# Layer norms on GpSimd: (y - mean) * rstd instead of y * rstd + (-mean * rstd), and one fence fewer per norm

## The chip, the core and the metric

The kernel runs on one core of a Trainium2 chip. The core has TensorE (matmuls), VectorE (DVE), ScalarE (ACT), GpSimd (POOL), and SyncE (SP), which here issues the DMAs. Each has an instruction queue of its own, worked off in order; they meet through semaphores. The metric is the device time of one execution in microseconds.

## The reference

The input x is [64, 128, 256] fp32 (64 graphs of 128 nodes with 256 features), adj a [64, 128, 128] integer mask. First comes a masked attention with 8 heads, `x = norm(x + relu(attention(x)) @ Wo)`. Then three GNN layers, each for every graph:

```python
scores = si[:, :, None] + sj[:, None, :] + attn_b[l]      # si, sj = x @ two halves of attn_w[l]
attn = softmax(where(mask, leaky_relu(scores), -inf))
h = layernorm(x + attn @ x, g1[l], beta1[l])
ff = gelu(h @ W1[l] + b1[l]) @ W2[l] + b2[l]
x = layernorm(h + ff, g2[l], beta2[l])
```

and at the end `out = norm(x0 + x)`, with x0 the result of the attention. Every norm is `(y - mean) / sqrt(var + 1e-5)` over the 256 features.

## The kernel before, in words

The 64 graphs are worked in groups of 4 (GROUP), so there are 16 groups. A tile of a group is [128 nodes, 4 graphs, 256 features]. The first stage ("attention") goes through the 16 groups. The second ("GNN") has 48 steps: t = 0 to 15 is layer 1, 16 to 31 layer 2, 32 to 47 layer 3 (the last). x goes from layer to layer through DRAM (`hist`): a step loads its group's x and stores the new one.

There are four kinds of norms, all on GpSimd, each for the 4 graphs of a group at once: after the attention (`ln_group`, tiles y, mv, xo; 16 times), norm 1 (`ln_attention`, from y1 to n1, then hb = n1 * g1 + (beta1 + b2); 48 times), norm 2 (`ln_ffn`, from y2 to norm, then * g2, + beta2 into xo; 48 times), and in the last layer the final norm (`final_norm`, fin; 16 times). DVE makes means and variances (bn_stats, bn_aggr) and puts them as (mean, variance) pairs into mv, mv1, mv2, mv3. GpSimd then runs `layernorm_on_pool` (lines 145 to 158): variance + eps (148), -mean (149), power -0.5 (151), the product -mean * rstd (153), a fence, and four big `tensor_scalar` instructions, one per graph of 256 elements a partition, y * rstd + (-mean * rstd) (156). `hold_pool` (lines 140 to 143) is a fence: a wait, followed by a small tensor_tensor on one element, which goes ahead of an instruction that reads a scalar per partition. One stands before line 148 (on the semaphore of mv), one before line 156; in ln_attention a further one is on hT_made.

The order of each engine's work in a GNN step t is written out by hand:
- GpSimd (`body`, line 781 on): norm 1 and hb of step t+1, in the last layer the final norm of t-1, norm 2 and xo of t.
- TensorE: transposes of the probabilities of t+1 (line 799), FFN 1 of t in 8 parts (line 45), with the aggregation of t+1 between them (807), FFN 2 of t in 4 blocks (line 834), in the middle of the third of which n1 of t+1 is transposed (821). A block of FFN 2 needs the bank which `residual2` on DVE (line 1003) has read two blocks before.
- DVE: the low parts of gelu (1011), residual 1 and its statistics of t+1, the attention sums of t+3 (`attention_sums`, line 940, two instructions for each of 4 graphs) between the calls of residual2 (1003), the low part of hT of t+1 (1016), the statistics of y2 (1007) and at the end mv2 (1101). The first attention sum of t+3 waits for its loads (g_ld), and residual2 of block 0 stands behind it.
- SyncE, layers 1 and 2: `load_ahead(t)` waits for y1 of t+1 and issues the four loads of step t+3 (x, mask, attn_w, attn_b; lines 123 to 128), `store_x(t)` waits for x_out, that is for xo of t, and stores it (line 689). So load_ahead(t) stands behind store_x(t-1). In the last layer store_out takes the place of store_x.
- ACT: gelu (917, 918), the exponentials (890, 891), hT (904, 905).

The matmuls are made from high and low parts of fp32 values, three products each.

Of the kernel before, what the change touches and what calls it, by code (L numbers as in the profile page):

```python
# [27 lines left out]
ALU = mybir.AluOpType  # L28
ACT = mybir.ActivationFunctionType

P = 128
GROUP = 4
EPS = 1e-5
# [16 lines left out]
def gnn_kernel(nc, x_in, adj, Wq, Wk, Wv, Wo, attn_w, attn_b, W1, b1, W2, b2, g1, beta1, g2, beta2, out):  # L50
    B, N, D = x_in.shape
# [27 lines left out]
    with ExitStack() as whole:  # L79
# [6 lines left out]
        sb, sems = tensor_maker(whole), sem_maker(whole)  # L86
# [6 lines left out]
        affine = sb("affine", [P, L, 5, D])  # L93
        b2_rows = sb("b2_rows", [P, L, D])
        half_neg = sb("half_neg", [P, GROUP])
        w1_raw = sb("w1_raw", [P, KT, F])
        w2_raw = sb("w2_raw", [P, FT, D])

        y = [sb(f"y{i}", [P, GROUP, D]) for i in range(2)]
        mv = [sb(f"mv{i}", [P, GROUP, 2]) for i in range(2)]  # L100
        inv = sb("inv", [P, 4, GROUP])
        xo = [sb(f"xo{i}", [P, GROUP, D]) for i in range(2)]

        XW = D + 2
# [6 lines left out]
        mv_out, ln_chain, ln_out = sems("mv_out", "ln_chain", "ln_out")  # L111
# [28 lines left out]
        def hold_pool(e, sem, value):  # L140
            e.wait_ge(sem, value)
            n = holds["pool"] = holds["pool"] + 1
            e.tensor_tensor(fence_pool[:, n:n + 1], half_neg[:, 0:1], half_neg[:, 0:1], ALU.add)  # L143

        def layernorm_on_pool(e, chain, n0, stats, inv, y, dest, done=None):


            e.tensor_scalar(inv[:, 0, :], stats[:, :, 1], EPS, None, ALU.add).then_inc(chain, 1)
            e.tensor_scalar(inv[:, 1, :], stats[:, :, 0], -1.0, None, ALU.mult).then_inc(chain, 1)
            e.wait_ge(chain, n0 + 1)  # L150
            e.tensor_tensor(inv[:, 2, :], inv[:, 0, :], half_neg[:], ALU.pow).then_inc(chain, 1)  # L151
            e.wait_ge(chain, n0 + 3)
            e.tensor_tensor(inv[:, 3, :], inv[:, 1, :], inv[:, 2, :], ALU.mult).then_inc(chain, 1)
            hold_pool(e, chain, n0 + 4)
            for j in range(GROUP):
                last = e.tensor_scalar(dest[:, j, :], y[:, j, 0:D], inv[:, 2, j:j + 1], inv[:, 3, j:j + 1],  # L156
                                       ALU.mult, ALU.add)
            last.then_inc(chain if done is None else done, 1)

        def ln_group(e, t, par):  # L160

            hold_pool(e, mv_out, t + 1)
            layernorm_on_pool(e, ln_chain, 4 * t, mv[par], inv, y[par], xo[par], ln_out)
            e.wait_ge(ln_out, START + t + 1)


        with ExitStack() as ctx:
            sb = tensor_maker(ctx, "att_")
# [109 lines left out]
            @block.gpsimd  # L278
            def _(e):
                e.memset(ident[:], 0.0).then_inc(eye_made, 1)  # L280
                e.wait_ge(eye_made, 1)
                e.affine_select(out=ident[:], in_=ident[:], compare_op=ALU.not_equal, fill=1.0, base=0,
                                pattern=[[-1, P]], channel_multiplier=1).then_inc(ident_set, 1)
                e.memset(half_neg[:], -0.5).then_inc(eye_made, 1)
                e.sem_inc(ln_out, START)
                e.wait_ge(eye_made, 2)
                e.wait_ge(ident_set, 1)

                def make_masks(q1, par, t1):

                    hold_pool(e, x_ld[par], 32 * (q1 + 1))
                    e.tensor_scalar(mask[par][:], adjl[par][:], 0.0, MASKED, ALU.is_equal, ALU.mult).then_inc(masks_made, 1)
                    e.tensor_scalar(adj_f[:], adjl[par][:], 1.0, None, ALU.mult).then_inc(eye_added, 1)
                    e.wait_ge(eye_added, 2 * t1 + 1)
                    for j in range(GROUP):
                        ins = e.tensor_tensor(eye_sum[:, j, :], adj_f[:, j, :], ident[:], ALU.add)
                    ins.then_inc(eye_added, 1)
                    hold_pool(e, eye_added, 2 * t1 + 2)
                    hold_pool(e, mask1_st[par], START + 16 * q1)
                    e.tensor_scalar(mask1[par][:], eye_sum[:], 0.0, MASKED, ALU.is_le, ALU.mult).then_inc(masks_made, 1)  # L300

                make_masks(0, 0, 0)

                e.wait_ge(const_ld, 16 * (5 + 3 * L))
                e.tensor_tensor(affine[:, :, 2, :], affine[:, :, 1, :], b2_rows[:], ALU.add).then_inc(aff_set, 1)

                def body(q, par, a1, a2):
                    t = 2 * q + par
                    if a1:
                        e.wait_ge(masks_made, 2 * (t + 1))  # L310
                        e.wait_ge(peaked, GROUP * t + 1)
                        make_masks(q + (par + 1) // 2, 1 - par, t + 1)
                    if isinstance(t, int) and t == NG - 1:
                        return
                    e.wait_ge(stored[par], START + 16 * q)
                    ln_group(e, t, par)

                steps(e, body)
# [270 lines left out]
        with ExitStack() as ctx:  # L589
            sb = tensor_maker(ctx, "gnn_")  # L590
# [138 lines left out]
            @block.gpsimd  # L729
            def _(e):  # L730
                for par in range(2):
                    e.memset(x[par][:, :, D:XW], 1.0).then_inc(x_ones, 1)
                e.wait_ge(stored[1], START + 16 * (NG // 2 - 1))
                ln_group(e, NG - 1, 1)
                e.sem_inc(norm2_out, START)
                e.sem_inc(fin_out, START)
                e.wait_ge(aff_set, 1)

                def row(l, n):
                    return affine[:, bass.ds(l, 1), n, :].rearrange("p o d -> p (o d)")  # L740

                def ln_attention(t1, par1):

                    l = layer_of(t1)
                    hold_pool(e, mv1_out, t1 + 1)
                    if not isinstance(t1, int):
                        hold_pool(e, hT_made, 2 * t1)
                    layernorm_on_pool(e, ln1, 5 * t1, mv1, inv, y1, n1, n1_out)
                    e.wait_ge(n1_out, t1 + 1)
                    for j in range(GROUP):  # L750
                        ins = e.tensor_tensor(hb[par1][:, j, :], n1[:, j, :], row(l, 0), ALU.mult)  # L751
                    ins.then_inc(ln1, 1)
                    e.wait_ge(ln1, 5 * t1 + 5)
                    for j in range(GROUP):
                        ins = e.tensor_tensor(hb[par1][:, j, :], hb[par1][:, j, :], row(l, 2), ALU.add)  # L755
                    ins.then_inc(hb_out, 1)
                    e.wait_ge(hb_out, t1 + 1)

                def ln_ffn(t, par, half, last_layer):

                    l = layer_of(t)
                    hold_pool(e, mv2_out, t + 1)
                    layernorm_on_pool(e, ln2, 5 * t, mv2, inv, y2, norm, norm2_out)
                    e.wait_ge(norm2_out, START + t + 1)
                    for j in range(GROUP):
                        ins = e.tensor_tensor(norm[:, j, :], norm[:, j, :], row(l, 3), ALU.mult)  # L766
                    ins.then_inc(ln2, 1)
                    e.wait_ge(ln2, 5 * t + 5)

                    e.wait_ge(stored[par], START + 16 * (T // 2 if last_layer else half + NG // 2))  # L770
                    for j in range(GROUP):
                        ins = e.tensor_tensor(xo[par][:, j, :], norm[:, j, :], row(l, 4), ALU.add)  # L772
                    ins.then_inc(x_out, 1)
                    e.wait_ge(x_out, t + 1)

                def final_norm(t1, par1):
                    hold_pool(e, mv3_out, t1 - FIRST + 1)
                    layernorm_on_pool(e, ln3, 4 * (t1 - FIRST), mv3, inv, fin[par1], fin[par1], fin_out)
                    e.wait_ge(fin_out, START + t1 - FIRST + 1)

                def body(q, par, more, layer_end, final):
                    if more >= 1:
                        t1, p1, _ = ahead(q, par, 1)
                        ln_attention(t1, p1)
                    if final:
                        t1, p1, _ = ahead(q, par, -1)
                        final_norm(t1, p1)
                    ln_ffn(2 * q + par, par, q, final or isinstance(q, int))

                ln_attention(0, 0)  # L790
                steps(e, body, peel_last_layer=True)
                final_norm(T - 1, 1)
# [364 lines left out]
```

## Time and profile before

| | us |
|---|---|
| median of 3 runs | 1864.64 (1861.49 to 1866.35) |
| the profiled execution, its own time | 1871.55 |
| its span, first to last instruction | 1869.6 |
| attention stage | about 0 to 440 |
| GNN layers 1 and 2 | about 440 to 1415 |
| layer 3 with the final norm | about 1415 to 1866 |

How to read it: busy is the time in which an engine executes. The idle time before an instruction is put down to what released it ("<-"). A line of the chain of waits is one piece of the path that ended last: its start, its length, its engine and tile. The number after x counts instructions. The granted clock of TensorE is given as a share of the full 2.4 GHz, so 0.50 is 1.2 GHz.

### The profile page before, as it was taken

Reading aid. Unit: us, or ns where it says so; the run is one execution under the profiler, and the core shown is the slowest. Engines: PE = TensorE matmul, PEld = TensorE weight load, DVE = VectorE, ACT = ScalarE, POOL = GpSimd, SP = SyncE. Lnnn points to the kernel's source line nnn. Section 1 sums busy time; section 2 is a strip of 40 time slices with the busy share of each in tenths; the row PEclk is TensorE's granted clock in tenths of the full one; section 3 lists DMA queues with packets and bytes.
Section 4 is the critical chain, followed back from the end, with each engine's and each line's share of the span. In section 5 each row is a group of like instructions: output and inputs, shape, how many; then the busy total and the mean of one; then the engine's idle time right before and its main releaser. Section 6 shows DMA issues by size and latency. Waiting matters only on the chain.

```text
span 1869.6 us, 40745 instructions
## 1 busy us (share of the span) xinstructions
PE 1670.7 (89%) x12032; PEld 1475.7 (79%) x12032; DVE 1379.5 (74%) x5414; ACT 1206.6 (65%) x2814; POOL 1269.8 (68%) x2260
## 2 busy tenths in 40 slices
PE   5999999974999999998899999999988999999995
PEld 4777877863888888888788888888877888887894
DVE  2888888887776777667766776677676887777873
ACT  3888888873665666656555666666656666666662
POOL 3255555533676766767566866766767999998996
PEclk8999999995999999999989999999999999999997
DMA  6222232332211212212131211212211222122111
GB/s 183 63 89 81 84 90 90 90 97 85 74 49 52 67 34 67 61 40 68 34 97 49 67 46 55 67 34 67 67 34 57 68 68 90 59 76 73 66 42 45
DMA packets 152115, 127.39 MB, mean 68 GB/s; under 512 B 16512, under 2 KB 145024, under 8 KB 152064
## 3 DMA queue, kind: packets, MB, share of 16 engines
q1 hardware_dynamic: 145024, 124.30, 21.6%
q10 hardware_dynamic: 7040, 2.51, 0.5%
q8 instruction: 19, 0.31, 0.1%
q14 instruction: 32, 0.26, 0.0%
HBM read 89.04 MB, written 37.75 MB: 68 GB/s over the span
## 4 chain that ended last, share of the span: by engine, by line
PE 28%; POOL 17%; DVE 9%; issue 8%; DMA 7%; SPq 4%; ACT 3%; POOLq 0%; ACTq 0%; DVEq 0%
PE ps L834 13%; PE ps L45 10%; DMA ab<-in_L_gnn_attn_b 7%; POOL xo L772 5%; POOL gnn_norm L766 4%; POOL gnn_norm L156 4%; DVE gnn_junk L940 3%; PE ps L821 3%; POOL inv L151 2%; DVE gnn_st L1007 2%; DVE gnn_res L1003 2%; PE ps L807 2%; SPq L124 1%; SPq L126 1%; SPq L689 1%
## 5 line engine op out<-in xcount | busy, mean ns | idle before, releaser
L834 PE MATMUL ps<-gnn_w_hi,gnn_g_hi 128*128 128x256 f32 x1536 | 446.6, 291 | 70.7 <-DVE gnn_res L1003 70.5
L834 PE MATMUL ps<-gnn_w_lo,gnn_g_hi 128*128 128x256 f32 x1536 | 435.6, 284 | 0.0
L834 PE MATMUL ps<-gnn_w_hi,gnn_g_lo 128*128 128x256 f32 x1536 | 435.3, 283 | 0.0
L143 POOL TENSOR_TENSOR fence_pool<-half_neg 128x1 f32<-128x1 f32 x346 | 65.8, 199 | 501.4 <-DVE gnn_mv L1101 235.3
L917 ACT ACTIVATE gnn_g_hi<-ps,b_cols 128x512 fp32r<-128x512 f32 x384 | 264.6, 689 | 211.8 <-PE ps L45 211.7
L1011 DVE TENSOR_TENSOR gnn_g_lo<-ps,gnn_g_hi 128x512 fp32r<-128x512 f32 x384 | 263.0, 685 | 161.7 <-ACT ps L918 161.6
L834 PEld LDWEIGHTS ps<-gnn_w_hi,gnn_g_hi 128*128 128x128 f32 x1536 | 296.0, 193 | 81.3 <-DVE gnn_res L1003 78.8
L45 PE MATMUL ps<-gnn_hT_hi,gnn_w_hi 128*128 128x512 f32 x768 | 341.1, 444 | 3.9 <-DVE gnn_g_lo L1011 3.9
L45 PE MATMUL ps<-gnn_hT_lo,gnn_w_hi 128*128 128x512 f32 x768 | 305.6, 398 | 0.0
L45 PE MATMUL ps<-gnn_hT_hi,gnn_w_lo 128*128 128x512 f32 x768 | 305.5, 398 | 0.0
L940 DVE CUSTOM_DVE_ANT_0 gnn_junk<-x,aw 128x256 f32<-128x256 f32 x384 | 213.1, 600 | 120.6 <-DMA ab<-in_L_gnn_attn_b 120.1
L834 PEld LDWEIGHTS ps<-gnn_w_lo,gnn_g_hi 128*128 128x128 f32 x1536 | 296.3, 193 | 2.2
L834 PEld LDWEIGHTS ps<-gnn_w_hi,gnn_g_lo 128*128 128x128 f32 x1536 | 295.6, 192 | 0.0
L918 ACT ACTIVATE ps<-ps,b_cols 128x512 f32<-128x512 f32 x384 | 250.7, 653 | 0.0
L904 ACT ACTIVATE gnn_hT_hi<-ps,beta_cols,g_cols 128x512 fp32r<-128x512 f32 x96 | 74.7, 779 | 218.5 <-PE ps L821 218.5
L443 ACT ACTIVATE att_probs<-att_probs,att_neg_peak 128x128 f32<-128x128 f32 x512 | 199.1, 394 | 7.8 <-DVE att_neg_peak L524 7.8
L45 PEld LDWEIGHTS ps<-gnn_hT_hi,gnn_w_lo 128*128 128x128 f32 x768 | 145.9, 190 | 35.0
L45 PEld LDWEIGHTS ps<-gnn_hT_hi,gnn_w_hi 128*128 128x128 f32 x768 | 145.9, 190 | 32.9 <-DVE gnn_g_lo L1011 4.8
L45 PEld LDWEIGHTS ps<-gnn_hT_lo,gnn_w_hi 128*128 128x128 f32 x768 | 146.3, 191 | 28.1
L755 POOL TENSOR_TENSOR gnn_hb<-gnn_hb,affine 128x256 f32<-128x256 f32 x192 | 154.7, 835 | 6.9 <-POOL gnn_hb L751 5.7
L751 POOL TENSOR_TENSOR gnn_hb<-gnn_n,affine 128x256 f32<-128x256 f32 x192 | 147.2, 799 | 8.6 <-POOL gnn_n L156 7.2
L772 POOL TENSOR_TENSOR xo<-gnn_norm,affine 128x256 f32<-128x256 f32 x192 | 135.6, 738 | 8.3 <-POOL gnn_norm L766 7.1
(120 smaller groups left out, 3882.5 us busy)
## 6 DMA issues: line engine op xcount, KB each, us to landing
hist<-xo SPq DMA_DIRECT2D x48, 512.0 KB, 3.3
x<-hist SPq DMA_DIRECT2D x48, 512.0 KB, 4.2
gmask<-mask_hist SPq DMA_DIRECT2D x48, 256.0 KB, 4.2
aw<-in_L_gnn_attn_w SPq DMA_DIRECT2D x48, 256.0 KB, 4.1
att_xq<-in_x SPq DMA_DIRECT2D x16, 512.0 KB, 4.6
att_xl<-in_x SPq DMA_DIRECT2D x16, 512.0 KB, 3.6
gnn_fin<-hist SPq DMA_DIRECT2D x16, 512.0 KB, 3.9
out<-gnn_fin SPq DMA_DIRECT2D x16, 512.0 KB, 3.0
```

Source lines behind the costliest of these rows:

```text
L45: last = pe.matmul(out, w_of(w[a], k), x_of(x[b], k), start=(n == 0 and k == 0), stop=(n == len(terms) - 1 and k == 1))
L156: last = e.tensor_scalar(dest[:, j, :], y[:, j, 0:D], inv[:, 2, j:j + 1], inv[:, 3, j:j + 1], ALU.mult, ALU.add)
L443: ins = e.activation(probs[b][:, h, :], probs[b][:, h, :], ACT.Exp, bias=neg_peak[b][:, h:h + 1], scale=SCALE, accum_out=den[b][:, h:h + 1])
L751: ins = e.tensor_tensor(hb[par1][:, j, :], n1[:, j, :], row(l, 0), ALU.mult)
L755: ins = e.tensor_tensor(hb[par1][:, j, :], hb[par1][:, j, :], row(l, 2), ALU.add)
L766: ins = e.tensor_tensor(norm[:, j, :], norm[:, j, :], row(l, 3), ALU.mult)
L772: ins = e.tensor_tensor(xo[par][:, j, :], norm[:, j, :], row(l, 4), ALU.add)
L834: mm = e.matmul(FF2[j % 2], g[a][:, m, j * N:(j + 1) * N], V[b][:, m, :], start=(n == 0), stop=(n == len(terms) - 1))
L917: e.activation(g[0][:, m, :], FF1[FFB[m]], ACT.Gelu, bias=bias)
L918: e.activation(FF1[FFB[m]], FF1[FFB[m]], ACT.Gelu, bias=bias).then_inc(gelu_out, 1)
L940: ins = e.tensor_tensor_reduce(out=junk[:, j, n, :], in0=x[par2][:, j, 0:D], in1=aw[par2][:, n, :], scale=1.0, scalar=0.0, op0=ALU.mult, o ...
L1011: e.tensor_tensor(g[1][:, m, :], FF1[FFB[m]], g[0][:, m, :].bitcast(F32), ALU.subtract).then_inc(g_lo_out, 1)
```

## The change

layernorm_on_pool adds eps by a tensor_tensor with a constant tile (eps, set once at the start), takes the power, and computes (y - mean) * rstd with the mean straight from the statistics tile. The negated mean and its product with rstd are left out, so the small tile inv has 2 rows instead of 4. The fence ahead of the first small instruction becomes a plain wait, since that instruction no longer is a tensor_scalar. In ln_attention the fence on hT_made becomes a plain wait too, and stands ahead of the one on mv1. The fence ahead of the four big instructions stays. The counts on the chain semaphores follow.

```diff
+        eps = sb("eps", [P, GROUP])
-        inv = sb("inv", [P, 4, GROUP])
+        inv = sb("inv", [P, 2, GROUP])
...
         def layernorm_on_pool(e, chain, n0, stats, inv, y, dest, done=None):
-            e.tensor_scalar(inv[:, 0, :], stats[:, :, 1], EPS, None, ALU.add).then_inc(chain, 1)
-            e.tensor_scalar(inv[:, 1, :], stats[:, :, 0], -1.0, None, ALU.mult).then_inc(chain, 1)
+            e.tensor_tensor(inv[:, 0, :], stats[:, :, 1], eps[:], ALU.add).then_inc(chain, 1)
             e.wait_ge(chain, n0 + 1)
-            e.tensor_tensor(inv[:, 2, :], inv[:, 0, :], half_neg[:], ALU.pow).then_inc(chain, 1)
-            e.wait_ge(chain, n0 + 3)
-            e.tensor_tensor(inv[:, 3, :], inv[:, 1, :], inv[:, 2, :], ALU.mult).then_inc(chain, 1)
-            hold_pool(e, chain, n0 + 4)
+            e.tensor_tensor(inv[:, 1, :], inv[:, 0, :], half_neg[:], ALU.pow).then_inc(chain, 1)
+            hold_pool(e, chain, n0 + 2)
             for j in range(GROUP):
-                last = e.tensor_scalar(dest[:, j, :], y[:, j, 0:D], inv[:, 2, j:j + 1], inv[:, 3, j:j + 1],
-                                       ALU.mult, ALU.add)
+                last = e.tensor_scalar(dest[:, j, :], y[:, j, 0:D], stats[:, j, 0:1], inv[:, 1, j:j + 1],
+                                       ALU.subtract, ALU.mult)
...
         def ln_group(e, t, par):
-            hold_pool(e, mv_out, t + 1)
-            layernorm_on_pool(e, ln_chain, 4 * t, mv[par], inv, y[par], xo[par], ln_out)
+            e.wait_ge(mv_out, t + 1)
+            layernorm_on_pool(e, ln_chain, 2 * t, mv[par], inv, y[par], xo[par], ln_out)
...
+                e.memset(eps[:], EPS)
                 e.memset(half_neg[:], -0.5).then_inc(eye_made, 1)
...
                 def ln_attention(t1, par1):
-                    hold_pool(e, mv1_out, t1 + 1)
                     if not isinstance(t1, int):
-                        hold_pool(e, hT_made, 2 * t1)
-                    layernorm_on_pool(e, ln1, 5 * t1, mv1, inv, y1, n1, n1_out)
+                        e.wait_ge(hT_made, 2 * t1)
+                    e.wait_ge(mv1_out, t1 + 1)
+                    layernorm_on_pool(e, ln1, 3 * t1, mv1, inv, y1, n1, n1_out)
...
                 def ln_ffn(t, par, half, last_layer):
-                    hold_pool(e, mv2_out, t + 1)
-                    layernorm_on_pool(e, ln2, 5 * t, mv2, inv, y2, norm, norm2_out)
+                    e.wait_ge(mv2_out, t + 1)
+                    layernorm_on_pool(e, ln2, 3 * t, mv2, inv, y2, norm, norm2_out)
...
                 def final_norm(t1, par1):
-                    hold_pool(e, mv3_out, t1 - FIRST + 1)
-                    layernorm_on_pool(e, ln3, 4 * (t1 - FIRST), mv3, inv, fin[par1], fin[par1], fin_out)
+                    e.wait_ge(mv3_out, t1 - FIRST + 1)
+                    layernorm_on_pool(e, ln3, 2 * (t1 - FIRST), mv3, inv, fin[par1], fin[par1], fin_out)
```

## Rows read from the trace of the kernel before

**Rows 1.** Page, busy us of each engine, share of the span, instructions.
```profile
PE 1670.7 (89%) x12032; PEld 1475.7 (79%) x12032; DVE 1379.5 (74%) x5414; ACT 1206.6 (65%) x2814; POOL 1269.8 (68%) x2260
```
**Rows 2.** Waits, 500 to 1400 us: who for whom, total us, times, longest.
```profile
POOL fence_pool L143 <- DVE gnn_mv L1101: 219.7, 31, 12.0
...
DVE gnn_junk L940 <- DMA ab<-in_L_gnn_attn_b: 113.2, 31, 6.5
...
PE ps L834 <- DVE gnn_res L1003: 65.5, 31, 4.2
```
**Rows 3.** Chain of waits, 1230 to 1251 us: start, length, what.
```profile
1230.60 2.84 POOL xo L772 x4
...
1233.61 0.41 SPq L689
...
1236.54 3.95 DMA ab<-in_L_gnn_attn_b
...
1242.21 0.35 DVE gnn_res L1003
...
1250.42 0.29 DVE gnn_mv L1101 x3
```
**Rows 4.** Waits, 60 to 440 us, the attention stage.
```profile
POOL fence_pool L143 <- DVE mv L533: 167.9, 15, 21.2
```
**Rows 5.** Timeline of one norm 2 on GpSimd: start, length.
```profile
1222.86 0.20 POOL L143 TENSOR_TENSOR fence_pool<-half_neg 128x1 f32<-128x1 f32 x1 [5.58 <-DVE gnn_mv L1101]
...
1223.45 0.23 POOL L149 TENSOR_SCALAR inv<-gnn_mv 128x4 f32<-128x4 f32 x1
...
1223.64 1.04 POOL L151 TENSOR_TENSOR inv<-inv,half_neg 128x4 f32<-128x4 f32 x1
...
1224.75 0.20 POOL L153 TENSOR_TENSOR inv<-inv 128x4 f32<-128x4 f32 x1
...
1225.04 0.19 POOL L143 TENSOR_TENSOR fence_pool<-half_neg 128x1 f32<-128x1 f32 x1
...
1225.22 2.19 POOL L156 TENSOR_SCALAR gnn_norm<-gnn_res,inv 128x256 f32<-128x256 f32 x4
```
**Rows 6.** Windows: length, busy of PE PEld DVE ACT POOL, clock, DMA.
```profile
499.58:530.35 30.77, 27.15 (x165) 24.53 (x164) 19.29 (x72) 17.84 (x33) 19.80 (x38) 0.94 0.17 53
...
1264.64:1292.28 27.64, 26.07 (x170) 23.44 (x169) 20.26 (x72) 18.34 (x33) 20.09 (x38) 1.00 0.19 57
1292.28:1322.02 29.74, 27.90 (x172) 25.28 (x171) 20.92 (x75) 18.58 (x33) 20.87 (x38) 0.94 0.17 53
...
1351.91:1380.74 28.83, 26.28 (x172) 23.66 (x171) 20.45 (x75) 18.55 (x33) 20.62 (x38) 1.00 0.18 53
...
1299.50:1301.00 1.50, 1.50 (x9) 1.50 (x8) 1.50 (x6) 0.00 (x0) 1.50 (x2) 0.50 0.00 0
```
**Rows 7.** Groups by line on GpSimd: busy us, mean ns.
```profile
L156 POOL TENSOR_SCALAR gnn_norm<-gnn_res,inv 128x256 f32<-128x256 f32 x192 | 108.2, 578 | 0.0
...
L300 POOL TENSOR_SCALAR att_mask<-att_eye_sum 128x512 f32<-128x512 f32 x16 | 31.0, 1935 | 1.1
...
L293 POOL TENSOR_SCALAR att_adj_f<-att_adjl 128x512 f32<-128x512 int32 x16 | 24.3, 1520 | 1.3
```
**Rows 8.** Last layer: chain, timeline of DVE and GpSimd, one window.
```profile
1712.82 2.17 issue
...
1737.57 0.95 DVE L940 CUSTOM_DVE_ANT_0 gnn_junk<-x,aw 128x256 f32<-128x256 f32 x1
...
1742.49 0.42 DVE L940 CUSTOM_DVE_ANT_0 gnn_junk<-x,aw 128x256 f32<-128x256 f32 x1
...
1736.64 4.04 POOL L755 TENSOR_TENSOR gnn_hb<-gnn_hb,affine 128x256 f32<-128x256 f32 x4
...
1528.30:1556.60 28.30, 26.29 (x170) 23.50 (x169) 23.05 (x83) 18.45 (x32) 26.36 (x48) 1.00 0.23 75
```
**Rows 9.** Timeline of GpSimd, the last norm's first instruction.
```profile
1861.57 0.19 POOL L143 TENSOR_TENSOR fence_pool<-half_neg 128x1 f32<-128x1 f32 x1 [3.36 <-DVE gnn_mv L1035]
```

More of the change, by code:

```diff
@@ L752, in ln_attention @@
                     ins.then_inc(ln1, 1)
-                    e.wait_ge(ln1, 5 * t1 + 5)
+                    e.wait_ge(ln1, 3 * t1 + 3)
                     for j in range(GROUP):
@@ L767, in ln_ffn @@
                     ins.then_inc(ln2, 1)
-                    e.wait_ge(ln2, 5 * t + 5)
+                    e.wait_ge(ln2, 3 * t + 3)
                     e.wait_ge(stored[par], START + 16 * (T // 2 if last_layer else half + NG // 2))
```

## The prediction, as it stood before the result was known

> **What bounds the kernel now.** I read the busy shares first, then the waits between 500 and 1400 us, then the chain of waits over one step, then windows cut step by step. The shares alone mislead: TensorE is busy 89% of the span and GpSimd 68% [rows 1], so one would call the kernel TensorE-bound and GpSimd free. The waits of the first two GNN layers say otherwise. GpSimd waits 31 times for mv2 (219.7 us together), DVE waits 31 times for the DMA that loads a later step (113.2 us), and TensorE waits 31 times for residual2 on DVE (65.5 us, 2.1 us each time) [rows 2]. One wait of each kind per step is a ring, and the chain shows it closed [rows 3]: mv2 of step t-1 is done, GpSimd runs norm 2 and xo (last group from 1230.60), SyncE stores xo (1233.61), and only then, because it is behind that store in SyncE's queue, issues the loads for step t+3, of which the last starts at 1236.54 and takes 3.95 us. DVE takes its attention sums from that load, residual2 of block 0 stands behind them (1242.21), the third ffn2 block of TensorE stands behind residual2, and the rest of the step ends with mv2 at 1250.42. So every microsecond of norm 2 on GpSimd is a microsecond of the step, as long as TensorE still stalls.
>
> Two other stretches. In the attention stage GpSimd waits 167.9 us in 15 waits for mv [rows 4]; its norms are off the path there. In the last GNN layer no x is stored, so the ring is open; TensorE sets the pace and stalls once a step, where it waits for hT_lo on DVE: 2.17 us at 1712.82 [rows 8]. There GpSimd is busy 26.36 of 28.30 us [rows 8], nearly full, but has some slack. After the last ffn2 the end is serial: a final norm, norm 2, a final norm, all on GpSimd [rows 9].
>
> **The change, part by part.** The head of a norm, from the first fence to the first row of the big tensor_scalar, lasts 1225.22 - 1222.86 = 2.36 us [rows 5]. After the change it holds an add (tensor_tensor on 4 elements: the product of that size and kind takes 0.20), a gap of 0.07 for the wait on it (1224.68, the power's end, to 1224.75 before the product), the power 1.04, a gap of 0.09 (before the second fence) and that fence, 0.19: 1.59 us. That is 0.77 us less per norm [rows 5]. What goes is the first fence, one tensor_scalar (0.23, partly under the power's start) and the product, each with its gap. Bounds: if the add cost as the small tensor_scalar does, 0.23, the gain is 0.74; if the gaps on both sides were zero it would be 0.93. The eps memset is one instruction at the start, beside the first loads: nothing. In ln_attention a second fence goes as well, behind the same semaphores in another order; nothing stands between the two waits, so their order costs nothing.
>
> The four big instructions change from (mult, add) to (subtract, mult). They take 578 ns on average now [rows 7]. The trace shows no subtract on GpSimd, and this is the unknown that matters. From below: nothing can be read off that would make it cheaper than the 562 ns that the undisturbed group of four gives, 2.19 us with its overlaps [rows 5]; the same loop, one input, two arithmetic operations, one output. From above: a tensor_scalar with (is_le, mult) on 512 elements takes 1935 ns, half of it 968 for 256; with one mult on an int32 input 1520, half 760 [rows 7]. The first contains a comparison and the second an integer input, which neither version of the norm does, so the nearest row by operands (fp32 in, two pointer scalars, two arithmetic operations) is the present one. I take the same price, and keep 968 as the other end. Break-even for the norm is 562 + 770/4 = 755 ns.
>
> The Trainium skill (GPSIMD Engine Reference, Performance pitfalls for Q7 kernels) says an fp32 dependent chain costs 4 cycles an element; at its clock 256 elements would then take an estimated 853 ns, and the norm would get 0.4 us longer, some 12 us over the ring. The present (mult, add) pair, which depends in the same way, takes 562 ns [rows 5], against that rule; whether (subtract, mult) does, no row shows.
>
> *Ring.* 31 norm-2 heads by 0.77 us: 23.9 us. Nothing comes up behind it: the TensorE stall of 2.1 us [rows 2] falls to 1.3 and still is one; norm 1 then starts when its own mv1 is there, and ends earlier too, but the transposes that read it are held by residual2, so this counts for nothing here.
>
> *Clock.* The 28 whole steps between 499.58 and 1380.74 (the layer change left out) are of two kinds: 15 with the clock at 1.00 take 28.04 us on average, 13 at 0.94 take 29.95 (the first and the last of them in [rows 6]). In a slow one the clock is at 0.50, that is 1.2 instead of 2.4 GHz, just after the stall [rows 6]. It costs 1.9 us each, 24.8 us in all. TensorE's idle time differs by tenths between them (29.74 - 27.90 = 1.84 us against 27.64 - 26.07 = 1.57 in two neighbours [rows 6]), so we sit at an edge; with 0.8 us less idle time I expect most of these falls to go, but since I can't tell from the rows which, I put half in the sum: 12.4 us. Bounds: 0 and 24.8.
>
> *Last layer.* Three norms a step give GpSimd 2.3 us of slack more, which TensorE does not need. But hb on GpSimd (L755, 4.04 us [rows 8], where an undisturbed group of that form takes 2.84 [rows 3]) runs at the same time as DVE's sums, which then take 0.95 us instead of 0.42 [rows 8]. L755 starts 0.77 us earlier, plus a fence, so about one of the two slowed sums gets free: 0.5 us earlier hT_lo, and with it the stall, in 12 steps: about 5 us with what that may spare in clock. Bounds: -12 (all sums freed, or a slow step or two saved) and +5 (the collision only moves to sums nearer to hT_lo).
>
> *Start and end.* The attention norms are hidden by the 168 us of waiting; if that cover were gone it would be 16 x 0.77 = 12 us more gain, no loss. In the tail three heads are serial (the last of them in [rows 9]): 2.3 us.
>
> Sum: 23.9 + 12.4 + 5 + 2.3 = 43.6 us. The profiled execution took 1871.55 us (span 1869.6 and 2 around it), so it would take 1828; the runs shown have their median 6.9 below it, at 1864.64, which gives 1821. With all of the clock's share and of the last layer it is 1800, with none of both 1838.
>
> **Rivals.** *First, the clock still falls.* The stall is shorter but the engine is still idle once a step, and it sits at an edge already. For it: slow and fast steps have almost the same idle time now. Against it: of the two neighbours the one with less has the clock at 1.00 [rows 6]. Time: 1864.6 - 23.9 - 2.3 = 1838.
>
> *Second, the slower side: (subtract, mult) runs in a dearer loop on GpSimd.* At 968 ns a norm gets 4 x 0.41 - 0.77 = 0.87 us longer. In the ring 31 x 0.87 = 27 us. In the last layer GpSimd is not busy for 28.30 - 26.36 = 1.94 us of a step [rows 8] and gets 3 x 0.87 = 2.6 more work, so it becomes the bound, by at least 0.7 us: 13 steps, 9 us. Tail 2.6. Together 1903, and up to 25 more if the longer stalls drop the clock in the fast steps. It decides at 755 ns per instruction: at 760 (the int32 row) the time is that of before. For it: two of three kinds of tensor_scalar on this engine cost 3.0 to 3.8 ns per element [rows 7], and (mult, add) 2.2. Against it: both dearer rows have something (a comparison, an integer) that this one lacks.
>
> *Third, nothing to be seen.* What the change saves on GpSimd another arrival takes back: DVE's sums in the ring collide with L751 and L755, and as the load lands 0.8 us earlier relative to mv2 it might meet more of them. Both groups move with it, and sums are slowed already, so little can be taken. 1865 at most, if a step loses 0.8 us on it.
>
> **How the numbers follow.** A measurement of this kernel can tell about 0.3%, 5.6 us, from no change. Forecast with part or all of the clock's share 0.50; first rival (1838) 0.18; a price between 600 and 755 ns, so a small gain, 0.05; third rival and a price at break-even 0.04; slower side 0.23. Faster is 0.50 + 0.18 + 0.05 less a little: 0.72; same 0.05; slower 0.23. The likeliest case alone runs from 1802 to 1842. The range has to take in part of the second rival until 2 in 10 are left out: above 1885 lie about 0.15, below 1802 about 0.05.
>
> **What would show it.** Head of norm 2 from the add to the first row of the big instruction at 1.6 us; the group of four at 2.19 us again (3.0 or more would be the second rival); steps in layers 1 and 2 of 27.3 us where the clock holds (28.04 - 0.77), TensorE's wait for residual2 at 1.3 us instead of 2.1; fewer windows at 0.94; in the last layer the stall before probs_T under 1.7 us; the end 2.3 us shorter. I am wrong in the mechanism if the steps keep 28 to 29.9 us with the head at 1.6; wrong in price if the group of four is over 2.4.

## The result: 8.9% slower, and the profile after

The changed kernel takes 2029.39 us (median, 2028.96 to 2030.27), beside 1863.07 for the kernel before: ratio 1.0886, 95% interval 1.0869 to 1.0903 (the quotient of the two medians is 1.0893). The forecast was 1821 and the range 1802 to 1885; it was wrong in sign.

The page of the changed kernel, busy time by engine, beside [rows 1]:

```profile
PE 1720.2 (85%) x12032; PEld 1527.9 (75%) x12032; DVE 1408.1 (69%) x5414; ACT 1205.6 (59%) x2814; POOL 1535.1 (76%) x1835
```

GpSimd issues 425 instructions fewer and is busy 265 us longer. The timeline of one norm 2 on GpSimd, which answers to [rows 5] (start, length, instruction):

```profile
1225.62 0.20 POOL L148 TENSOR_TENSOR inv<-gnn_mv,eps 128x4 f32<-128x4 f32 x1 [6.52 <-DVE gnn_mv L1099]
1225.90 1.03 POOL L150 TENSOR_TENSOR inv<-inv,half_neg 128x4 f32<-128x4 f32 x1
1227.01 0.19 POOL L144 TENSOR_TENSOR fence_pool<-half_neg 128x1 f32<-128x1 f32 x1
1227.19 4.84 POOL L153 TENSOR_SCALAR gnn_norm<-gnn_res,gnn_mv,inv 128x256 f32<-128x256 f32 x4
...
1232.21 2.82 POOL L764 TENSOR_TENSOR gnn_norm<-gnn_norm,affine 128x256 f32<-128x256 f32 x4 [0.18 <-POOL gnn_norm L153]
```

The head came out as forecast: 1227.19 - 1225.62 = 1.57 us, against 2.36 before. The four big instructions take 4.84 us instead of 2.19. By line, for all of them (busy us, mean ns), beside [rows 7]:

```profile
L153 POOL TENSOR_SCALAR gnn_norm<-gnn_res,gnn_mv,inv 128x256 f32<-128x256 f32 x192 | 234.7, 1235 | 0.0
```

One instruction is 1235 ns on average, 578 before, and in the final norm, the lowest of the four kinds, 1221. So a norm is 4.84 + 1.57 - 2.19 - 2.36 = 1.86 us longer.

Waits of the changed kernel, 500 to 1400 us (who for whom, total us, times, longest), beside [rows 2]:

```profile
POOL inv L148 <- DVE gnn_mv L1099: 158.7, 28, 11.5
DVE gnn_junk L938 <- DMA ab<-in_L_gnn_attn_b: 152.6, 28, 8.3
...
PE ps L832 <- DVE gnn_res L1001: 106.2, 28, 6.4
```

TensorE's wait for residual2 is now 3.8 us a step instead of 2.1, and 28 steps fit where 31 did. Windows of two neighbouring steps, a stretch of layers 1 and 2, and one of the last layer (length, busy of PE PEld DVE ACT POOL, clock, DMA), beside [rows 6, 8]:

```profile
1208.67:1241.15 32.48, 28.71 (x169) 26.09 (x168) 21.79 (x72) 18.32 (x32) 24.22 (x30) 0.89 0.17 49
1241.15:1272.39 31.24, 27.90 (x171) 25.29 (x170) 21.84 (x72) 18.55 (x34) 25.18 (x32) 0.95 0.16 50
1650.00:1950.00 300.00, 252.94 (x1514) 229.60 (x1513) 198.00 (x723) 165.87 (x289) 288.10 (x334) 0.91 0.19 60
```

Both steps shown are below full clock; before, 15 of 28 were at 1.00. In the last layer GpSimd is busy 96% of the time and TensorE 84%. TensorE's waits there (1650 to 1950 us) name the same engine:

```profile
PEld ps L819 <- issue: 48.6, 9, 6.2
PE ps L819 <- POOL gnn_n L153: 47.1, 9, 6.0
```

It waits 5 us a step for n1, a wait that [rows 8] has no match for: there the stall was on hT_lo. In the same window norm 1's own big instructions take 1651 ns on average, those of the other two norms 1222 and 1223.

Where the 158.1 us between the two spans lie, by the times at which SyncE issues the loads of x. Each trace has a list of 46 such times, counted from 0: number 0 is the load of step 2, number 2 that of step 4, number 34 that of step 36. The steps below are differences of neighbours in it.

| | before | after | difference |
|---|---|---|---|
| start to number 2 | 497.4 | 499.8 | +2.4 |
| layers 1 and 2, number 2 to number 34 | 942.6 | 1025.0 | +82.4 |
| mean of 28 steps in it | 28.93 | 31.68 | +2.75 |
| the rest: last layer and tail | 429.6 | 502.9 | +73.3 |
| mean of 9 steps in it, number 35 to 44 | 28.7 | 33.2 | +4.5 |

### The profile page after: what moved, and what is told of

Read it like the earlier page. It is cut to its first block, busy times and chain, and to the rows that moved or that the text cites. A ratio compares the mean times of both kernels' runs of the same rounds, so it can differ in the third digit from the quotient of the medians.

```text
span 2027.7 us, 40233 instructions
## 1 busy us (share of the span) xinstructions
PE 1720.2 (85%) x12032; PEld 1527.9 (75%) x12032; DVE 1408.1 (69%) x5414; ACT 1205.6 (59%) x2814; POOL 1535.1 (76%) x1835
## 4 chain that ended last, share of the span: by engine, by line
POOL 41%; PE 11%; DVE 7%; issue 7%; DMA 7%; SPq 4%; ACT 1%; POOLq 1%; DVEq 0%; ACTq 0%
POOL gnn_norm L153 12%; PE ps L832 8%; POOL xo L770 7%; DMA ab<-in_L_gnn_attn_b 7%; POOL gnn_norm L764 6%; POOL gnn_n L153 4%; POOL inv L150 4%; POOL gnn_fin L153 3%; PE ps L819 2%; POOL gnn_hb L749 2%; POOL gnn_hb L753 2%; DVE gnn_junk L938 2%; DVE gnn_st L1005 1%; DVE gnn_res L1001 1%; SPq L125 1%
## 5 line engine op out<-in xcount | busy, mean ns | idle before, releaser
L832 PE MATMUL ps<-gnn_w_hi,gnn_g_hi 128*128 128x256 f32 x1536 | 466.3, 304 | 123.1 <-DVE gnn_res L1001 123.1
L832 PE MATMUL ps<-gnn_w_lo,gnn_g_hi 128*128 128x256 f32 x1536 | 454.2, 296 | 0.0
L832 PE MATMUL ps<-gnn_w_hi,gnn_g_lo 128*128 128x256 f32 x1536 | 453.0, 295 | 0.0
L832 PEld LDWEIGHTS ps<-gnn_w_hi,gnn_g_hi 128*128 128x128 f32 x1536 | 315.8, 206 | 131.9 <-DVE gnn_res L1001 129.6
L938 DVE CUSTOM_DVE_ANT_0 gnn_junk<-x,aw 128x256 f32<-128x256 f32 x384 | 246.7, 687 | 182.6 <-DMA ab<-in_L_gnn_attn_b 182.2
L832 PEld LDWEIGHTS ps<-gnn_w_lo,gnn_g_hi 128*128 128x128 f32 x1536 | 315.9, 206 | 2.2
L832 PEld LDWEIGHTS ps<-gnn_w_hi,gnn_g_lo 128*128 128x128 f32 x1536 | 315.0, 205 | 0.0
L153 POOL TENSOR_SCALAR gnn_n<-gnn_res,gnn_mv,inv 128x256 f32<-128x256 f32 x192 | 251.0, 1319 | 0.0
L153 POOL TENSOR_SCALAR gnn_norm<-gnn_res,gnn_mv,inv 128x256 f32<-128x256 f32 x192 | 234.7, 1235 | 0.0
L148 POOL TENSOR_TENSOR inv<-gnn_mv,eps 128x4 f32<-128x4 f32 x112 | 25.2, 225 | 239.7 <-DVE gnn_mv L1099 187.4
```

The lines of the kernel that those rows point to most:

```text
L153: last = e.tensor_scalar(dest[:, j, :], y[:, j, 0:D], stats[:, j, 0:1], inv[:, 1, j:j + 1], ALU.subtract, ALU.mult)
L832: mm = e.matmul(FF2[j % 2], g[a][:, m, j * N:(j + 1) * N], V[b][:, m, :], start=(n == 0), stop=(n == len(terms) - 1))
L938: ins = e.tensor_tensor_reduce(out=junk[:, j, n, :], in0=x[par2][:, j, 0:D], in1=aw[par2][:, n, :], scale=1.0, scalar=0.0, op0=ALU.mult, o ...
```

## The experiments

Step means below are taken in the same way, over the same 28 steps of layers 1 and 2 (and 9 of the last). In the comparisons the kernel before took 1863.1 to 1867.1 us.

### 1. What does one instruction cost?

```diff
+                e.tensor_scalar(scr_o[:, 0:256], scr_a[:, 0:256], scr_s[:, 0:1], scr_s[:, 1:2], ALU.mult, ALU.add).then_inc(menu, 1)
+                e.wait_ge(menu, 3)
...
```

> The kernel before, with 32 more tensor_scalar instructions on GpSimd ahead of the first mask, each alone (it waits for the one before it), on fp32 tiles of 256 elements (two pairs also on 64), every form twice. Theory A (the pair of operations decides: mult then add has a fast loop, any other pair a slow one): (mult, add) 560 ns, (subtract, mult) 1220 ns, with immediates as with scalars from a tile; on 64 elements the difference shrinks to a quarter, some 165 ns. Theory B (the operand decides: a scalar read from the statistics tile with its stride of two elements, or two scalars from different tiles): (subtract, mult) with both scalars from one packed tile is 560 ns too. Theory C (a fixed extra cost per instruction): the difference is 660 ns at 64 elements as well. Of the pairs that could serve a norm, (add, mult) and (mult, subtract), A as stated gives 1220 ns.

Groups by line of that kernel (busy us, mean ns). A second input `att_scr_s` means that the scalars come from a tile; without it they are immediates. The pairs, in the order of the rows, are (mult, add), (add, mult), (subtract, mult), (add, add), mult alone, subtract alone; with immediates (mult, add), (subtract, mult), (is_le, mult), mult alone; and on 64 elements (mult, add), (subtract, mult):

```profile
L309 POOL TENSOR_SCALAR att_scr_o<-att_scr_a,att_scr_s 128x256 f32<-128x256 f32 x1 | 0.6, 554 | 0.1
...
L317 POOL TENSOR_SCALAR att_scr_o<-att_scr_a,att_scr_s 128x256 f32<-128x256 f32 x1 | 0.6, 554 | 0.1
...
L315 POOL TENSOR_SCALAR att_scr_o<-att_scr_a,att_scr_s 128x256 f32<-128x256 f32 x1 | 1.2, 1224 | 0.1
...
L331 POOL TENSOR_SCALAR att_scr_o<-att_scr_a,att_scr_s 128x256 f32<-128x256 f32 x1 | 1.2, 1218 | 0.1
...
L343 POOL TENSOR_SCALAR att_scr_o<-att_scr_a,att_scr_s 128x256 f32<-128x256 f32 x1 | 0.9, 917 | 0.1
...
L347 POOL TENSOR_SCALAR att_scr_o<-att_scr_a,att_scr_s 128x256 f32<-128x256 f32 x1 | 0.9, 922 | 0.1
...
L335 POOL TENSOR_SCALAR att_scr_o<-att_scr_a 128x256 f32<-128x256 f32 x1 | 0.4, 404 | 0.1
...
L339 POOL TENSOR_SCALAR att_scr_o<-att_scr_a 128x256 f32<-128x256 f32 x1 | 1.1, 1068 | 0.1
...
L359 POOL TENSOR_SCALAR att_scr_o<-att_scr_a 128x256 f32<-128x256 f32 x1 | 1.1, 1067 | 0.1
...
L351 POOL TENSOR_SCALAR att_scr_o<-att_scr_a 128x256 f32<-128x256 f32 x1 | 0.8, 848 | 0.1
...
L367 POOL TENSOR_SCALAR att_scr_o<-att_scr_a,att_scr_s 128x64 f32<-128x64 f32 x1 | 0.4, 399 | 0.1
...
L371 POOL TENSOR_SCALAR att_scr_o<-att_scr_a,att_scr_s 128x64 f32<-128x64 f32 x1 | 0.6, 579 | 0.1
```

Theory A holds, B and C fall: both scalars came from one packed tile, and the difference is 180 ns at 64 elements and 670 at 256. From 64 to 256 elements (mult, add) grows by 155 / 192 = 0.81 ns per element, (subtract, mult) by 645 / 192 = 3.36. But A's "any other pair" was too wide: (add, mult) is as fast as (mult, add). The other forms that were measured with DVE idle are slow, one operation alone too (917 against 554 for two). Two scalars from a tile cost 150 to 156 ns more than two immediates, fast or slow; one scalar costs 69 to 76 more.

Two pairs have no price. (mult, subtract) took 1562 and 2004, (mult, mult) 1036 and 1396. These four instructions ran from 7.34 to 13.64 us, and of the whole list they alone had company on DVE:

```profile
7.96 0.69 DVE L569 CAST att_w_hi<-att_w_raw 128x1024 fp32r<-128x1024 f32 x1 [7.96 <-DMA att_w_raw<-in_L_gnn_Wk]
...
11.75 1.46 DVE L571 TENSOR_TENSOR att_w_lo<-att_w_raw,att_w_hi 128x1024 fp32r<-128x1024 f32 x1
```

So whether these two pairs are fast or slow stays open.

### 2. One word in the instruction, from either side

```diff
-                last = e.tensor_scalar(dest[:, j, :], y[:, j, 0:D], stats[:, j, 0:1], inv[:, 1, j:j + 1],
-                                       ALU.subtract, ALU.mult)
+                last = e.tensor_scalar(dest[:, j, :], y[:, j, 0:D], inv[:, 1, j:j + 1], stats[:, j, 0:1],
+                                       ALU.mult, ALU.add)
```

> The changed kernel with the operations of the four big instructions alone exchanged: (mult by rstd, add mean), same tiles and the same two scalars. It computes y * rstd + mean, so this leaves the subtraction of the mean out. Theory A (operations): the group of four takes 2.19 us again and the shorter head of a norm shows alone: the sum of the prediction without the price of the subtract, 1821 us (1802 to 1842). Theory B (operands): the group stays at 4.84 us and the time at 2029.

Measured: 1816.24 us (1815.02 to 1818.96), ratio to before 0.9745 (0.972 to 0.977). The big instructions of norm 2 are at 572 ns, the step at 27.11 us. The sum of the prediction without its one wrong price (1821) is 5 us off. This kernel leaves the subtraction of the mean out; experiment 6 has one that computes the norm in full and takes as long (1815.03).

The other side is the kernel before with this edit:

```diff
-                last = e.tensor_scalar(dest[:, j, :], y[:, j, 0:D], inv[:, 2, j:j + 1], inv[:, 3, j:j + 1],
-                                       ALU.mult, ALU.add)
+                last = e.tensor_scalar(dest[:, j, :], y[:, j, 0:D], stats[:, j, 0:1], inv[:, 2, j:j + 1],
+                                       ALU.subtract, ALU.mult)
```

> The kernel before with (y - mean) * rstd in the four big instructions and nothing else changed: the negated mean and the product are still computed, all fences stay. Theory A: the group takes 4.84 us, and the kernel is slower than the changed one by what the shorter heads save, some 0.77 us in each of 31 norms of the ring, 3 x 0.77 us in each of the 16 steps of the last layer where GpSimd is the bound: 2029 + 24 + 37 = 2090 us. Theory B (something else in the change, fences or the order of waits, makes it slow): at most half of the 166 us, below 1946.

Measured: 2086.40 us (2084.60 to 2094.59), ratio 1.1186 (1.1158 to 1.1214). So the pair costs 221 us on the old head and 213 on the new one, and the new head saves 49 or 57. Nothing else in the change makes it slower.

### 3. Is norm 2 in a ring through SyncE's queue?

```diff
+                load_ahead(0, 0)
                 with e.Fori(0, L - 1) as l:
...
-                            load_ahead(l * pairs + p, par)
+                            load_ahead(l * pairs + p + par, 1 - par)
                             store_x(l * pairs + p, par)
                 first = (L - 1) * pairs
-                load_ahead(first, 0)
                 load_ahead(first, 1)
```

> The kernel before with one thing moved in SyncE's queue: in layers 1 and 2 the loads of a step stand ahead of the store of the x before it, so they wait for y1 alone and no longer for norm 2 on GpSimd. If norm 2, store, load and attention sums are the ring that sets the step, the loads start 2 us earlier, TensorE's wait for residual2 (2.1 us a step) goes or shrinks to under 0.5, fewer steps have the lower clock, and the time falls by 40 to 85 us, to 1780 to 1825. If the ring is not what holds TensorE, nothing moves (1863).

Measured: 1785.23 us (1780.51 to 1787.74), ratio 0.9578 (0.9551 to 0.9605); the step 26.35 us. Waits of that kernel, 500 to 1400 us:

```profile
DVE gnn_junk L940 <- DMA ab<-in_L_gnn_attn_b: 2.3, 9, 0.4
...
DVE gnn_res L1003 <- PE ps L834: 0.4, 2, 0.2
PEld ps L834 <- DVE gnn_res L1003: 0.2, 1, 0.2
```

The 65.5 us of TensorE's wait and the 113.2 us of DVE's [rows 2] are gone. The same move on the changed kernel:

> The changed kernel, (subtract, mult) in all norms, with the loads ahead of the store in SyncE's queue. Ring theory: in layers 1 and 2 the dear norm 2 is no longer on the path and GpSimd's own work, 2 x (4.84 + 1.6) + 4 x 2.9 = 24.5 us, is less than TensorE's 26.3 of a step, so these layers run at 26.6 to 27.5 us instead of 31.7: 130 to 155 us less, while the last layer stays bound by GpSimd: 1875 to 1900. Rival (the dear instruction slows DVE and TensorE by contention wherever it runs): the gain is no more than what the same move brought before, 80 us, 1949.

Measured: 1874.25 us (1871.90 to 1878.65), ratio to before 1.0041 (1.0023 to 1.0058). The step is 26.80 instead of 31.68 us, the last layer stays at 33.2. That is at the lower edge of what was expected, and far from the rival's 1949. With the ring open the dear pair costs little in layers 1 and 2: 26.80 - 26.35 = 0.45 us a step beside before_loads_first, which has the longer head, and 26.80 - 25.90 = 0.90 beside add_mult_loads_first (experiment 6), which has the short one. TensorE's only wait on GpSimd there is for n1, 0.7 us a step (500 to 1300 us):

```profile
PE ps L819 <- POOL gnn_n L153: 21.3, 29, 1.4
```

The 155 us that this move brings are twice what it brought before.

### 4. Which norm costs what?

The edit is in a flag: (subtract, mult) in one kind of norm, (mult, add) in the others, which leave the subtraction of the mean out.

```diff
-                    layernorm_on_pool(e, ln2, 3 * t, mv2, inv, y2, norm, norm2_out)
+                    layernorm_on_pool(e, ln2, 3 * t, mv2, inv, y2, norm, norm2_out, sub=True)
```

> The run after_mult_add with (subtract, mult) in norm 2 alone; norm 1, the final norm and the attention's norm keep (mult by rstd, add mean), which leaves the subtraction of the mean out there. Ring theory: 4 x 0.665 = 2.66 us more in each of 31 steps of layers 1 and 2 = 82 us, up to 25 us more by a lower clock, nothing in the last layer (GpSimd has room for one dear norm of three), 2.7 in the tail: 1816 + 85 to 110 = 1901 to 1926. Rival (cost is spread evenly over norms, because GpSimd as a whole is the bound): the same as norm 1 alone, about a third to 0.4 of 213 us, some 1890 for both.

> The run after_mult_add with (subtract, mult) in norm 1 alone, the other norms keep (mult by rstd, add mean). Ring theory: norm 1 is off the ring and its result is there 7 us before TensorE transposes it, GpSimd idles 5 us before norm 2, so layers 1 and 2 don't move; in the last layer GpSimd has room for one dear norm. Same as after_mult_add within 0.5%: 1810 to 1830. Rival (GpSimd as a whole is the bound): some 1890.

> The run after_mult_add with (subtract, mult) in the final norm alone, the others keep (mult by rstd, add mean). It runs only in the last layer, 16 times. GpSimd has 200 - 169.7 = 30 us to spare in 200 there, 4.2 us a step, and one dear norm needs 2.66, so by occupancy nothing but the tail is lost: 2 x 2.66 = 5 us, 1821. By collision (it pushes norm 2 and hb): up to 1 us a step more, 1837.

| (subtract, mult) in | us | above after_mult_add | step in layers 1, 2 | step in the last |
|---|---|---|---|---|
| none (after_mult_add) | 1816.24 | | 27.11 | 28.1 |
| norm 2 | 1974.54 (1970.66 to 1975.37) | 158 | 31.74 | 29.3 |
| norm 1 | 1864.31 (1861.69 to 1871.30) | 48 | 28.05 | 29.6 |
| final norm | 1820.21 (1816.50 to 1828.19) | 4 | 27.21 | 28.3 |
| all | 2029.39 | 213 | 31.68 | 33.2 |

Norm 2 as expected in kind, but dearer than 1901 to 1926: 2.67 us of added length make a step 4.63 us longer. Norm 1 not as expected: I had it at nothing. The final norm at 4, as expected by occupancy, though the runs of the two kernels overlap, so 4 us is not told from nothing. In layers 1 and 2 norm 1 adds nothing once norm 2 is dear (31.68 against 31.74). In the last layer each norm alone costs 0.2 to 1.4 us a step and all together 5.1: there the engine fills up, 96% busy in the changed kernel.

### 5. Length or contention?

For norm 1, small instructions that move next to no data take the place of the dear ones, behind n1 and ahead of hb:

```diff
                     e.wait_ge(n1_out, t1 + 1)
+                    for n in range(2):
+                        e.tensor_tensor(pad[:, n, :], half_neg[:], half_neg[:], ALU.add)
+                        e.tensor_tensor(pad[:, 2 + n, :], eps[:], half_neg[:], ALU.pow)
```

> The run after_mult_add (the subtraction of the mean left out as there) with four small instructions on GpSimd (two adds, two powers on 4 elements, some 2.5 us together, hardly a byte moved) between n1, which is already signalled, and hb. It tells why sub_norm1_only was 48 us slower than after_mult_add. Collision theory: the delay pushes the two hb groups next to DVE's attention sums, which share the port, DVE hands over hT_lo later and the ring gets longer: 0.8 to 1.1 us in each of 31 steps and 1 us a step in the last layer, 1850 to 1865, with the mean attention sum at 0.75 to 0.80 us instead of 0.60. Lateness theory (n1 itself came too late for TensorE): n1 is not delayed here, so 1816 to 1822.

Measured: 1848.53 us (1845.56 to 1855.83), 32 above after_mult_add and a little below the expected 1850 to 1865; step 28.11 us, as with the dear norm 1 (28.05). Attention sums on DVE, 1000 to 1300 us, in after_mult_add, in this kernel and in sub_norm1_only (busy us, mean ns):

```profile
L938 DVE CUSTOM_DVE_ANT_0 gnn_junk<-x,aw 128x256 f32<-128x256 f32 x88 | 49.1, 602 | 26.7 <-DMA ab<-in_L_gnn_attn_b 26.7
```
```profile
L942 DVE CUSTOM_DVE_ANT_0 gnn_junk<-x,aw 128x256 f32<-128x256 f32 x87 | 61.7, 752 | 29.4 <-DMA ab<-in_L_gnn_attn_b 29.4
```
```profile
L942 DVE CUSTOM_DVE_ANT_0 gnn_junk<-x,aw 128x256 f32<-128x256 f32 x88 | 66.1, 795 | 32.2 <-DMA ab<-in_L_gnn_attn_b 32.2
```

Eight sums a step by 0.15 us is 1.2 us on DVE, and n1 was not late. Nor was norm 2 held up: GpSimd still waits for mv2, 5.3 us a step (500 to 1300 us).

```profile
POOL inv L149 <- DVE gnn_mv L1103: 148.9, 28, 10.6
```

So it is the collision: a later hb meets the sums. Longer sums by themselves need not lengthen the step, where DVE does not stand in the ring: in before_loads_first they take 0.72 us, and its step is 26.35. In the last layer the delay did less than the dear norm (28.9 against 29.6); that rest, some 16 us of the 48 with the tail, I have not split further.

The same four instructions in norm 2, between the norm and the product with g2:

> The run after_mult_add with the same four small instructions in norm 2, between the big instructions and the product with g2: 2.5 us of delay in the ring without a dear instruction or data moved. Ring theory: it costs what (subtract, mult) in norm 2 cost, 158 us for 2.66 us, of which 31 x 2.66 = 82 are the time itself and the rest the lower clock in nearly every step: 1816 + 150 = 1950 to 1975. If the dear instruction hurts by more than its length (port contention with DVE), the delay alone costs clearly less: 1895 to 1920.

Measured: 1944.96 us (1942.19 to 1949.48), 129 above after_mult_add. Its timeline shows what the delay was:

```profile
1190.55 2.17 POOL L154 TENSOR_SCALAR gnn_norm<-gnn_res,inv,gnn_mv 128x256 f32<-128x256 f32 x4
1192.80 0.20 POOL L765 TENSOR_TENSOR pad<-half_neg 128x4 f32<-128x4 f32 x1
...
1194.07 1.01 POOL L766 TENSOR_TENSOR pad<-eps,half_neg 128x4 f32<-128x4 f32 x1
1195.05 2.82 POOL L768 TENSOR_TENSOR gnn_norm<-gnn_norm,affine 128x256 f32<-128x256 f32 x4
```

From 1192.72, where the big ones end, plus the usual 0.18, to 1195.05 is 2.15 us. The time is below the expected 1950 to 1975, as the delay came out shorter than the 2.5 us that I had assumed. The step grew by 3.80, 1.77 per microsecond of delay; the dear pair by 4.63 for 2.67, 1.73. So in the ring only length counts. The factor above 1 goes with the clock. Windows of 1000 to 1300 us in after_mult_add, delay_in_norm2 and sub_norm2_only:

```profile
1000.00:1300.00 300.00, 290.79 (x1862) 261.50 (x1861) 225.32 (x798) 205.30 (x358) 209.67 (x335) 1.00 0.19 58
```
```profile
1000.00:1300.00 300.00, 270.76 (x1627) 244.58 (x1625) 192.28 (x696) 180.39 (x315) 207.00 (x336) 0.94 0.17 52
```
```profile
1000.00:1300.00 300.00, 264.48 (x1580) 240.63 (x1581) 188.57 (x680) 170.86 (x296) 193.82 (x272) 0.92 0.16 47
```

Scaled to one step, TensorE is idle 0.83, 3.01 and 3.76 us and busy 26.28, 27.90 and 27.98 (estimates from these windows and the mean steps). The idle time grows by the added length, and the same matmuls take 1.6 to 1.7 us longer at the lower mean clock.

### 6. A version that beats both

```diff
+            e.tensor_tensor(inv[:, 2, :], stats[:, :, 0], minus[:], ALU.mult)
...
-                last = e.tensor_scalar(dest[:, j, :], y[:, j, 0:D], stats[:, j, 0:1], inv[:, 1, j:j + 1],
-                                       ALU.subtract, ALU.mult)
+                last = e.tensor_scalar(dest[:, j, :], y[:, j, 0:D], inv[:, 2, j:j + 1], inv[:, 1, j:j + 1],
+                                       ALU.add, ALU.mult)
```

> The changed kernel with the big instructions as (y + (-mean)) * rstd, a pair that took 554 ns alone; -mean comes from one more small tensor_tensor between the add of eps and the power, so a head has one instruction of 0.2 us more. Theory A (only the pair was dear): group of four at 2.19 us, head 1.6 + 0.15 to 0.25 us, time 1816 + 31 x 0.2 = 1822 to 1830, faster than before by 2%. Rival (a subtraction or the statistics operand costs in some other way): over 1863.

Measured: 1815.03 us (1812.01 to 1815.89), ratio to before 0.9724 (0.970 to 0.9748). The change's idea, with an addition for the subtraction, is 2.8% faster than before. The extra instruction costs less than expected (1822 to 1830), since it runs where the power waited for the add:

```profile
1184.68 0.20 POOL L149 TENSOR_TENSOR inv<-gnn_mv,eps 128x4 f32<-128x4 f32 x1 [6.51 <-DVE gnn_mv L1102]
1184.83 0.20 POOL L150 TENSOR_TENSOR inv<-gnn_mv,minus 128x4 f32<-128x4 f32 x1
1184.99 1.01 POOL L152 TENSOR_TENSOR inv<-inv,half_neg 128x4 f32<-128x4 f32 x1
...
1186.26 2.17 POOL L155 TENSOR_SCALAR gnn_norm<-gnn_res,inv 128x256 f32<-128x256 f32 x4
```

The power starts 0.31 us after the add, against 0.28 without the extra one.

> Both improvements in one kernel: (y + (-mean)) * rstd with the short head, and the loads ahead of the store. Layers 1 and 2 are already bound by TensorE in before_loads_first (26.3 us a step), so the shorter head brings nothing there; the last layer, the layer changes and the tail gain some 0.2 us a step and 2 us: 1775 to 1786, against 1785 of before_loads_first. If the stall at the start of a last-layer step stays as it is, same as before_loads_first.

Measured: 1771.08 us (1769.12 to 1774.32), ratio to before 0.9497 (0.9471 to 0.9522), the best of all, and 4 us below the expected stretch: layers 1 and 2 did gain, 25.90 us a step against 26.35, where I had expected nothing.

## Why the prediction was wrong, by its own steps

**The step that failed** is the price of the four big instructions: "I take the same price". It is 1221 to 1235 ns, not 562, and lay outside the bound of 968 as well. Three errors are in it.
- "The nearest row by operands" compared inputs, scalars and the number of operations. What decides is which two operations: (mult, add) and (add, mult) were fast, (subtract, mult), (add, add) and (is_le, mult) were not.
- The upper bound halved a duration: 1935 ns for 512 elements is not 968 for 256, because a part of it is per instruction. The small tensor_scalar (L149, 0.23 us [rows 5]) gives that part: (1935 - 230) / 2 + 230 = 1083 ns, and 1067 to 1077 were measured for that pair on 256 elements. The rows had this, though the small instruction has one operation and 4 elements, so that it comes so near is in part luck: by the two sizes of experiment 1 the part per instruction is 208 ns with immediates (1068 - 256 x 3.36).
- The bound's row has immediates, the norm has scalars from a tile, 150 ns more, so about 1220. Those 150 no row before the change showed.

The Trainium skill (GPSIMD Engine Reference, Performance pitfalls for Q7 kernels) has 4 cycles an element for an fp32 dependent chain, by its clock an estimated 853 ns for 256. The slope measured for (subtract, mult) agrees: 3.36 ns an element, where 4 cycles at the page's 1.2 GHz are an estimated 3.33. I had weighed the rule without a part per instruction; with the 364 ns that the two sizes leave (579 - 64 x 3.36) it gives an estimated 1217 ns, and 1224 was measured. That the dependence is the cause is not shown: (mult, add) depends in the same way, grows by 0.81 ns an element and takes 554.

**The other steps.** The head: 0.77 us forecast, 0.79 measured (2.36 - 1.57). The ring: right, shown by opening it (3) and by a pure delay (5). But "every microsecond of norm 2 on GpSimd is a microsecond of the step" put too little on it: a microsecond of delay cost 1.77, one of the dear pair 1.73 (5). The size of what the head saves: 43.6 forecast, 49 measured in after_mult_add. Its clock share was halved out of caution and was more than whole: the step fell by 1.82 us, 0.77 of it the head, and the clock of 500 to 900 us rose from 0.97 to 1.00. The 1.05 left are 33 us over 31 steps, above the bound of 24.8. The first rival, by which the clock would still fall (1838), is out with that. The last layer: 0.6 us a step, near the 0.5 assumed. The attention stage, "12 us more gain, no loss": the norms themselves were hidden, but the first load of x in the GNN stage came at 449.5 instead of 441.2 us in after_mult_add and add_mult, at 447.8 in before_sub_mult, and at 440.7 in the changed kernel. The loss builds up through the stage: between 70 and 364 us a group takes 24.5 us in after_mult_add and 24.0 before. Its cause stays open. So that 1821 lies 5 us from 1816.24 is in part luck. In the profiled executions layers 1 and 2 gave 57 us instead of 36.3 and the rest 7.6 instead of 7.3, and the start took 8.1 back.

**The slower rival** had the right mechanism, place and break-even (755 ns) and the wrong size, 1903 plus up to 25. At the measured price its terms would be 31 x 1.86 = 58 in the ring, where 82 were measured (the 25 us of clock that it named complete them), 13 x (3 x 1.86 - 1.94) = 47 in the last layer and 3 x 1.86 = 5.6 in the tail, where 73 were measured for both. In the last layer GpSimd has 3 x 6.4 + 4 x 2.8 = 30.4 us of its own work a step. Norm 1's four big instructions add 4 x (1.65 - 1.22) = 1.7 in the stretch from 1650 to 1950 us, and the rest up to 33.2 I have not split. I gave that rival 0.23 with a range that ended at 1885, on a price for which no row of the same operations existed. A cost that is multiplied by 512 and stands in a ring needed a range up to where its bound, rightly worked out, led: with 1220 ns the sum is 1864.6 + 57.7 + 47.3 + 5.6 = 1975, and 2000 with its clock share. That is still 29 short of the 2029 measured.

**Norm 1** "counts for nothing here": right for n1, wrong for hb, which comes after it on the same engine. Making norm 1 later moves hb into DVE's sums (48 us in experiment 4, some 30 of them in layers 1 and 2). The prediction had seen the collision in the last layer, and did not ask the same of layers 1 and 2.

## What to carry to other kernels

On GpSimd the price of a tensor_scalar goes by its pair of operations, so measure the pair in a small kernel before counting instructions, at a time when DVE is idle; y + (-m) for y - m is worth a small instruction. A row of another size must be split into a part per instruction and one per element before it serves as a bound. And look for what stands behind what in a DMA queue: one store ahead of a load made a norm on an engine that was idle a third of the time the pace of the kernel, and exchanging the two brought more (4.2%) than all the work on the norm (2.8%); together 5.0%.

## What the runs showed of the hardware

- GpSimd, fp32, 256 elements a partition, scalars from a tile: (mult, add) and (add, mult) 554 ns; (subtract, mult) and (add, add) about 1220; one operation alone 917 to 929. With immediates 404, 1068 (also for a comparison) and 848. One operation costs more than the fast pairs of two, and less than the slow ones.
- A stall of TensorE costs more than its length when the granted clock falls behind it: 1.73 to 1.77 us of step per us of delay in norm 2 here, with the mean clock of the stretch at 0.92 to 0.94 instead of 1.00. In the other direction, shortening the ring by 0.77 us brought 1.82.
- The attention sums of DVE (two inputs in SBUF) take 0.60 us on average in after_mult_add and 0.75 to 0.80 where hb on GpSimd comes 2 to 3 us later. With the loads first they take 0.42 on the changed kernel and 0.72 in before_loads_first.
